# Delta rule of a two-layer model: chain loop in blocks of 8 steps, and the W/U stage in three lagged parts with PSUM banks of their own

## What is computed

```python
def step(Sst, inp):
    q_t, k_t, v_t, b_t, g_t = inp
    Sst = Sst * g_t[..., None, None]
    kS = jnp.einsum('bhk,bhkv->bhv', k_t, Sst)
    Sst = Sst + b_t[..., None, None] * jnp.einsum('bhk,bhv->bhkv', k_t, v_t - kS)
    o_t = jnp.einsum('bhk,bhkv->bhv', q_t, Sst)
    return (Sst, o_t)
```

## Time and profile before

| | us |
|---|---|
| median of 3 runs | 5109.11 |
| the profiled execution, its own time | 5108.61 |
| its span, first to last instruction | 5106.9 |
| PE busy | 3737.7 (73%) |
| DVE busy | 2733.6 (54%) |
| ACT busy | 2108.3 (41%) |
| POOL busy | 1172.7 (23%) |
| mean granted TensorE clock | 0.837 |
| W/U stage (phase_mix), 3397.5 to 3636 | 238.5 |
| chain (phase_chain), 3641.8 to 4099.5 | 457.7 |

### The profile page before, as it was taken

One profiled execution on the slowest core, in us unless ns is written; L12 is line 12 of the kernel. 1 busy time (PEld: TensorE's weight loads), 2 busy tenths in 40 slices (PEclk: granted clock), 3 DMA queues, 4 the chain that ended last, 5 costly groups with the idle time before them and its releaser, 6 DMA issues. The chain is left out here.

```text
span 5106.9 us, 109157 instructions
## 1 busy us (share of the span) xinstructions
PE 3737.7 (73%) x37201; PEld 1984.0 (39%) x37203; DVE 2733.6 (54%) x5646; ACT 2108.3 (41%) x3466; POOL 1172.7 (23%) x2077
## 2 busy tenths in 40 slices
PE   6699999999999995528585447026444469789999
PEld 3233333333333332416363226016333346444478
DVE  5688888888888884812123654751133434423433
ACT  0177777777777774214242213013222212243322
POOL 4321121121122110162003730724200013311100
PEclk8799999999999997769797765557555579889999
DMA  1400000000000002044533323334433110040053
GB/s 44 168 35 0 0 0 0 0 0 0 0 0 0 0 0 78 25 156 152 173 119 103 116 84 122 90 106 161 86 42 46 23 56 4 11 157 25 4 186 131
DMA packets 256377, 319.78 MB, mean 63 GB/s; under 512 B 27729, under 2 KB 177489, under 8 KB 256209
## 3 DMA queue, kind: packets, MB, share of 16 engines
q1 hardware_dynamic: 243920, 283.86, 19.0%
q0 software_dynamic: 12288, 33.57, 2.0%
HBM read 181.58 MB, written 135.79 MB: 62 GB/s over the span
## 5 line engine op out<-in xcount | busy, mean ns | idle before, releaser
L791 DVE TENSOR_REDUCE att_maxes<-att_ps_m 128x1 f32<-128x512 f32 x2048 | 1342.0, 689 | 337.2 <-PE att_ps_m L648 324.0
L755 ACT ACTIVATE att_prob<-att_ps_s 128x1024 f32<-128x1024 f32 x1024 | 992.7, 1021 | 439.5 <-PE att_ps_s L658 429.5
L648 PE MATMUL att_ps_m<-att_k_t,att_q_t 96*128 96x512 bf16 x2048 | 792.8, 387 | 22.4 <-DVE att_maxes L791 4.8
L658 PE MATMUL att_ps_s<-att_q_t,att_k_t 99*128 99x512 bf16 x2048 | 612.6, 380 | 1.8 <-ACT att_q_t L741 1.7
L670 PE MATMUL att_ps_o<-att_prob,att_v_h 128*32 128x512 f32 x4096 | 546.3, 605 | 0.8 <-DVE att_o_sum L804 0.5
L648 PEld LDWEIGHTS att_ps_m<-att_k_t,att_q_t 96*128 96x128 bf16 x2048 | 196.6, 96 | 696.9 <-DVE att_maxes L791 595.0
L562 POOL CAST att_max_parts<-att_neg_max 128x4 bf16<-128x4 f32 x128 | 24.7, 193 | 1306.6 <-DVE att_neg_max L798 1306.6
L1359 DVE TENSOR_TENSOR experts_h<-experts_gs,experts_ps_g 128x128 f32<-128x128 f32 x192 | 55.4, 288 | 468.3 <-ACT experts_gs L1340 466.4
L658 PEld LDWEIGHTS att_ps_s<-att_q_t,att_k_t 99*128 99x128 bf16 x2048 | 190.7, 98 | 206.4 <-issue 31.7
L2209 ACT ACTIVATE chain_faded<-chain_state,chain_gam 128x32 f32<-128x32 f32 x512 | 126.6, 311 | 330.0 <-DVE chain_state L2233 320.6
L1312 PE MATMUL experts_ps_g<-w_gu,experts_x_t 128*128 x768 | 217.9, 406 | 35.6 <-ACT experts_x_t L1336 18.9
(11 more groups left out here) (346 smaller groups left out, 6398.5 us busy)
## 6 DMA issues: line engine op xcount, KB each, us to landing
slots_x<-zeros SPq DMA_DIRECT2D x97, 256.0 KB, 3.3
experts_xs<-slots_x SPq DMA_DIRECT2D x48, 512.0 KB
slots_y<-experts_y SPq DMA_DIRECT2D x48, 512.0 KB
logits_t<-sstat_logit SPq DMA_DIRECT2D x64, 256.0 KB
xf_t<-logits_t SPq DMA_DIRECT2D x8, 2048.0 KB
proj<-comb_pr SPq DMA_DIRECT2D x8, 1600.0 KB
mix_pr<-proj SPq DMA_DIRECT2D x32, 400.0 KB
w_d<-in_L_ffn_wd SPq DMA_DIRECT2D x2, 4096.0 KB, 20.0
```

The lines of the kernel that those rows point to most:

```text
L648: pe.matmul(ps_m[i % 2][:, :], q_t[0:PAIRS, p, tile * P:(tile + 1) * P], k_t[0:PAIRS, p, c * W:(c + 1) * W], start=True, stop=True).then_i ...
L658: mm = pe.matmul(ps_s[half][:, i * W:(i + 1) * W], k_t[0:ROWS, p, tile * P:(tile + 1) * P], q_t[0:ROWS, p, chunk * W:(chunk + 1) * W], sta ...
L755: nc.scalar.activation(prob[:, i % RING, :, :].rearrange("q a w -> q (a w)"), ps_s[half][:, :], ACT.Exp, scale=SCALE).then_inc(expd.sem, 1)
L791: v.tensor_reduce(maxes[:, p, tile, c:c + 1], ps_m[i % 2][:, :], X, ALU.max).then_inc(reduced.sem, 1)
```

## The change

In `phase_chain` CB becomes 8: there are 16 blocks, two to a pass, so eight passes, and each pass has half as much program text. Transfers and copies per block halve in size and double in number.

In `phase_mix`:
- loads, stores and the buffers that they touch get a ring of 4 (`LOADS`), and the loop body is 4 rounds long instead of 2;
- first products, second products and transposes get two PSUM banks each (`ps_x`, `ps_y`, `ps_t`), and PE has three stages, first(t), second(t - 1), turn(t - 2), so that a wait of one finds the others' work between;
- ACT widens the factors of the first and of the second products apart (two instructions of half size each instead of one of full size), in stages 0 and 2, and empties `ps_t` in stage 4; SP stores in stage 3;
- the small matmuls run over the heads in order, four quadrants each, and the four quadrants write one bank, where before they wrote four;
- the decay at each chunk's end is no longer widened and multiplied per tile (L1983, L2026, L2056 go, 32 times each line's work), but loaded once at the start with 64-byte rows, widened once by POOL, transposed by four transposes before tile 0, and copied once by ACT after the last tile.

The diff, cut to its core:

```diff
-    HG = H // 4
+    LOADS = 4
+    HALF = H // 2
...
-        ps = [ph.ps(f"ps{i}", [P, HG, GP]) for i in range(2)]
+        ps_x = [ph.ps(f"ps_x{i}", [P, GP]) for i in range(2)]
+        ps_y = [ph.ps(f"ps_y{i}", [P, GP]) for i in range(2)]
+        ps_t = [ph.ps(f"ps_t{i}", [P, GP]) for i in range(2)]
+        ps_e = ph.ps("ps_e", [P, GP])
...
+                sp.dma_start(ends[:, :, :], factors.rearrange("(i n t) a h -> n i t a h", i=B, t=CL)[:, :, CL - 1, 0, :]).then_inc(ends_in, 16)
             def load(t, p):
-                sp.wait_ge(scaled.sem, scaled.before(t))
+                sp.wait_ge(kv_scaled.sem, kv_scaled.before(t))
+                sp.wait_ge(qk_scaled.sem, qk_scaled.before(t))
-                sp.wait_ge(widened.sem, widened.before(t))
+                sp.wait_ge(wide_t.sem, wide_t.before(t))
+                sp.wait_ge(wide_p.sem, wide_p.before(t))
...
-            staged(sp, NT, load, idle, store)
+            staged(sp, NT, load, idle, idle, store, unroll=LOADS)
...
-            staged(pool, NT, scale)
+            staged(pool, NT, scale_kv, scale_qk, unroll=LOADS)
...
             def first(t, p):
-                pe.wait_ge(widened.sem, widened.at(t))
-                pe.wait_ge(scaled.sem, scaled.at(t, 3))
-                pe.wait_ge(w_q_kept.sem, w_q_kept.before(t))
+                pe.wait_ge(wide_t.sem, wide_t.at(t))
+                pe.wait_ge(kv_scaled.sem, kv_scaled.at(t))
+                pe.wait_ge(x_kept.sem, x_kept.before(t))
-                for n in range(HG):
-                    for i in range(4):
-                        for r in range(4):
-                            own, group = slice(32 * r, 32 * r + 32), (n + r) % HG
-                            h = 4 * group + i
-                            mm = pe.matmul(ps[p][own, group, 32 * i:32 * i + 32], ...
+                for h in range(H):
+                    for r in range(4):
+                        own = slice(32 * r, 32 * r + 32)
+                        mm = pe.matmul(ps_x[p % 2][own, 32 * h:32 * h + 32], ...
             def second(t, p):
                 pe.wait_ge(x_kept.sem, x_kept.at(t))
+                pe.wait_ge(wide_p.sem, wide_p.at(t))
+                pe.wait_ge(y_kept.sem, y_kept.before(t))
...
+            def turn(t, p):
                 pe.wait_ge(y_kept.sem, y_kept.at(t))
-                pe.wait_ge(scaled.sem, scaled.at(t, 5))
+                pe.wait_ge(w_q_kept.sem, w_q_kept.before(t))
...
-                for half in range(KD):
-                    mm = pe.matmul(ps[p][:, 1, half * CPT:(half + 1) * CPT], gam_k[...], ident[:, CL - 1:P:CL], ...
-            staged(pe, NT, first, second)
+            staged(pe, NT, first, second, turn, unroll=LOADS)
...
-            staged(act, NT, widen, keep_x, keep_w_q)
+            staged(act, NT, widen_t, idle, keep_x, idle, keep_w_q, unroll=LOADS)
...
-CB = 16
+CB = 8
```

More of the change, by code:

```diff
@@ L77, in before @@
     def before(self, t, p):
-        return t * (16 * self.per) + (32 - 16 * p) * self.per
+        step = 32 // self.ring
+        return t * (step * self.per) + (32 - step * p) * self.per
 def hold(eng, gate):
@@ L161, in steps, with transfers @@
         return Steps(self.sem(name), per, ahead)
-    def transfers(self, name, per=1, soft=False):
-        return Transfers([self.sem(f"{name}{p}", soft) for p in range(2)], per, soft)
+    def transfers(self, name, per=1, soft=False, ring=2):
+        return Transfers([self.sem(f"{name}{p}", soft) for p in range(ring)], per, soft)
     def block(self):
@@ L1918, in phase_mix @@
         y_kept = ph.steps("y_kept", 2)
-        turned = ph.steps("turned")
-        w_q_kept = ph.steps("w_q_kept", KD + 1)
-        stored = ph.transfers("stored", 2)
+        turned = ph.steps("turned", 1, LOADS)
+        w_q_kept = ph.steps("w_q_kept", KD)
+        stored = ph.transfers("stored", 2, ring=LOADS)
         block = ph.block()
@@ L1935, in _ @@
                 s.prime(sp)
+            with nc.allow_non_contiguous_dma("the decay at each chunk's end"):
+                sp.dma_start(ends[:, :, :], factors.rearrange("(i n t) a h -> n i t a h", i=B, t=CL)[:, :, CL - 1, 0, :]).then_inc(ends_in, 16)
             def load(t, p):
-                sp.wait_ge(scaled.sem, scaled.before(t))
+                sp.wait_ge(kv_scaled.sem, kv_scaled.before(t))
                 hold(sp, gate)
-                sp.wait_ge(widened.sem, widened.before(t))
+                sp.wait_ge(qk_scaled.sem, qk_scaled.before(t))
+                hold(sp, gate)
+                sp.wait_ge(wide_t.sem, wide_t.before(t))
+                hold(sp, gate)
+                sp.wait_ge(wide_p.sem, wide_p.before(t))
                 hold(sp, gate)
@@ L2009, in second @@
                 pe.wait_ge(x_kept.sem, x_kept.at(t))
+                pe.wait_ge(wide_p.sem, wide_p.at(t))
+                pe.wait_ge(y_kept.sem, y_kept.before(t))
                 hold(pe, gate)
[L2011 to L2017, removed]
+                for h in range(H):
+                    for r in range(4):
+                        own = slice(32 * r, 32 * r + 32)
+                        mm = pe.matmul(ps_y[p % 2][own, 32 * h:32 * h + 32], wide[own, p % 2, H + place(h), :, :].rearrange("q a t -> q (a t)"),
+                                       nat[own, p, 0:2, h, :], start=True, stop=True, skip_group_check=True)
                 mm.then_inc(seconds.sem, 1)
+            def turn(t, p):
                 pe.wait_ge(y_kept.sem, y_kept.at(t))
-                pe.wait_ge(scaled.sem, scaled.at(t, 5))
+                pe.wait_ge(w_q_kept.sem, w_q_kept.before(t))
                 for half in range(KD):
@@ L2046, in keep_x @@
                 for a in range(2):
-                    nc.scalar.copy(nat[:, p, a, :, :].rearrange("q (g h) d -> q g h d", g=HG),
-                                   ps[p][:, :, 0:P].rearrange("q g (h a d) -> q g h a d", a=2, d=HD)[:, :, :, a, :]).then_inc(x_kept.sem, 1)
+                    nc.scalar.copy(nat[:, p, a, :, :], ps_x[p % 2].rearrange("q (h a d) -> q h a d", a=2, d=HD)[:, :, a, :]).then_inc(x_kept.sem, 1)
+                act.wait_ge(seconds.sem, seconds.before(t))
+                widen(p, slice(H, 2 * H), wide_p)
             def keep_w_q(t, p):
```

106 lines of the change are left out of this document (61 added, 45 removed).

## The result

The changed kernel takes 5129.39 us (median of 6 executions, 5127.78 to 5136.92) where the kernel before, run beside it, took 5108.28: ratio 1.0044, 95% interval 1.0031 to 1.0056. It is 21 us slower; the forecast was 5000 us. Ratios leave out executions in a slower state at a lower granted clock, of which there was one, 5263.65 us at 0.757, of the kernel with two tiles per pass. The span of the profiled execution is 5127.2 us, the mean granted clock of TensorE 0.826.

The account below looks back on a forecast made before the run. It took PE's issue waits for refetched program text to bound the chain, and PE's waits for other engines to slow W/U. Chain -109 and W/U 0 gave 5000 us from 5108.6; range 4950 to 5185, its own 4970 to 5040.

Parts of the forecast that it names:

- The fetched text: Chain and W/U loops: bodies of about 8.4 packets of 16 KB, plain edge 2.1 us, refetching 7.8 us per pass.
- the overhang: Loop text beyond eight packet places: only packets sharing a place with it return, back-edge plus 1.5 edges, 7.8 us per pass.
- the side of the held: Chain and W/U loops: 2080 matrix instructions, nearer to attention's held 1284 (1.6) than the chain's 4096 (2.0), so text mostly stays.
- Rival 1: Chain and W/U loops: every packet fetched again, W/U +64, chain -9, together +55, 5164 us; chance 0.41.
- 35 of bursts: Chain, if every packet is fetched again: 35 us for long stalls falling together with block loads, within 436 us of run.
- First load 9 us: Chain start: the half-size first load, for which PE waits entirely, takes 9 us for 16.0 (8 to 12).
- POOL and SP at nothing: Chain: twice as many transfer issues on SP and copies on POOL cost nothing, as both run a block ahead.
- The waits of 1.33 and 1.08 go: W/U stage, per tile: PE's waits for DVE's copy (1.33 us) and ACT's emptying (1.08 us) vanish, inputs being a round old.
- Four quadrants now write one bank: W/U small matmuls: sharing one bank costs 0; the upper bound was a matmul's full 236 ns latency without overlap.
- PE's 4.5 us per tile: W/U stage: PE's time per tile from products 1.70 and 1.79, transposes 0.5, and about 0.5 for waits and holds.
- The transfer loop: W/U stage: store, next load, widening and products take 10 us over two rounds, so no tile under 5.0 us.
- mostly hidden: Skill's sentence on 16 KiB crossings, not used: would give chain -8, W/U 172 us (-66), 5034 us in all.

## Why the prediction was wrong

**The fetched text, the step that failed.** The prediction read the unit rightly (16 KB, 123 matmuls, an edge of 2.1 us), and that both new bodies are some 8.4 packets against a likely room of eight. The step that failed is "if a packet's place follows from its address, a body of 8.4 in eight places loses only those that share a place with the overhang", and the choice by ratio ahead of it, "I take the side of the held". Nine or ten packets came back in each pass, none was kept. The ratio 1.6 against 2.0 could not decide: what counts here is whether the packets number over eight, and by the division both bodies did. The ratio also left out waits and register work, with which attention's body is 1,526 instructions and still stays. What was left was overhang or all, and there the address was an assumption with no row behind it. A later pass of the chain takes 50.7 us ((4116.8 - 3761.6) / 7, from branch to branch), 19.0 above its 16 steps of 1.98, where I took 7.8. The Trainium skill ("Runtime: NRT & Kernel Launch", Instruction fetch mechanics) gives TensorE 2048 instructions as a FIFO. The trace agrees in that a body in nine packets keeps none and one in eight can be kept; the runs can't tell a FIFO from another rule that gives way to the oldest.

**Rival 1, what happened.** W/U +64 by its sum, +66 measured; 9.1 us per tile, (3679.4 - 3450.7) / 24 = 9.5 measured. Packets per pass "9 or 10": 9 and 10. Issue waits "170": 146.3. Its chain, -9, came out at -44, so the total was 5164 for 5129. The term mis-sized is "35 of bursts": carried over from the kernel before as if it belonged to the fetches, when it belonged to the block loads beside them. The rest of that sum, 253.4 + 114.7 + 32.6 = 400.7, meets the measured 401.0, with some luck: the edge at 2.1 us divided the whole remainder of 182.8 us, where the issue waits alone (175.2) give 1.95, and the changed chain has (146.3 - 7 x 4.2) / 60 = 1.95.

**Chain, other terms.** First load 9 us: 8.6 measured. POOL and SP at nothing: right in the changed kernel; with blocks of 4 POOL's copies show, 37.8 us.

**W/U, other terms.** "The waits of 1.33 and 1.08 go": they did (6.3 us of waits for other engines in 24 tiles; part of them may lie hidden under the waits for text). "Four quadrants now write one bank", priced at 0: right; the 128 first products still take 1.70 us from start to start in the kernel with the late copy, and a small matmul takes 237 ns for 236. PE's 4.5 us per tile was low: 9.5 less 91.0 / 24 = 3.8 of issue waits and 0.3 of others leave 5.5. A part of that are the transposes, 1.11 us for four at a granted clock of 0.50 in this stage, the lower of the two levels (1.2 GHz), where they took 0.65 in the kernel before with 0.75 on average. The transfer loop was 5.6 for 5.0. So even with no text to fetch the stage would, by an estimate from the kernel with two heads per matmul, have stood near 5.6 us per tile, about 32 x 5.6 + 12 = 191 us, -47, and not the -66 that the sentence on the skill's "mostly hidden" had. That sentence itself (same section) does not hold here: 53 waits in six W/U passes of the changed kernel cost 91 us.

**Range and chances.** The time lies within the range, but on the side that had 0.41. With a room of eight as its own guess and both bodies above it, the side of "all come back" deserved the larger chance: the one row of a body over eight, the chain's, kept nothing.

## What to carry to other kernels

Before a loop with many small matmuls is unrolled further, count the instructions of its longest engine, weight loads and waits included: here every body of up to 1,526 instructions stayed (but for a single packet in some loops), of two that lie in eight packets of 256 one stayed (1,782) and one did not (1,910), and those in nine or more lost all of them in every pass, at 1.4 to 2.0 us an edge on average and about 4 us for the back-edge. A pipeline that needs four rounds per pass can lose more to its text than to the waits that it removes; cutting the text of a pass to a quarter (blocks of 4 for 16 here, -169 us) is a change of one constant. Where such a loop can't be made to fit, keep large transfers of short rows away from it, since its packets of text wait behind them.

## What the runs showed of the hardware that I had not expected

- The loss is a step: the body of 1,782 instructions fetches nothing after its first pass, that of 2,038 fetches nine packets in every pass and has 220 us more of issue waits. The body of 1,910 fetches nine too.
- A body that lies in eight packets brought nine per pass (1,910 instructions, 18 behind an edge), and PE stood still for 4.7 to 5.3 us after its branch, where the same body with one packet at the branch took 3.4 to 4.0.
- The same body with the same nine packets has 57 us more of issue waits in another place (298 us for 241), and was 63 us slower in one execution each.
- A fetch is overlapped little: its transfer begins at most 0.6 us before PE stops in the changed chain and at most 1.7 us in its W/U stage, and PE goes on some 1.4 us after it has ended.
- Instruction packets wait behind data: 34.6 us of the kernel before, in eight stalls of up to 8.8 us, fell away when the block loads were thinned.
- The W/U stage in which PE stands still for its text is granted 0.50 for 0.75; the variant with half the instructions has 0.80. The chain is granted 0.50 with its text kept (blocks of 4) and without.
